# Vision tower on one Trainium2 core: the last two attention batches in pairs of tiles, and layer 1 of the FFN further ahead

## What is computed

```python
h = concatenate([cls_tok, tokens(x) @ W.T])                  # (8, 1025, 64)
e = layernorm(h)
S = (e @ WQ.T) @ (e @ WK.T).T / 8
P = exp(S - max(S)) * where(S == 0, 0, tril)                 # the max runs over the whole row
h = h + (P / (sum(P) + 1e-9)) @ (e @ WV.T)
x2 = layernorm(h)
w = softmax(mean(x2, axis=0) @ Wr + br)                      # one gate per token place, over all 8 batches
t = relu(bn2(relu(bn1(x2 @ W1[e])) @ W2[e]))                 # experts e = 0..7
out = h + sum_e w[:, e] * (t @ Wo[e] + bo[e])
```

## Time and profile before

| | |
|---|---|
| runs | 376.05, 377.1, 378.49 us |
| profiled execution | 379.81 us, its span 377.7 us |
| mean granted TensorE clock | 0.977 |
| TensorE busy | 355.9 us (94%) |
| VectorE busy | 269.9 us (71%) |
| ScalarE busy | 207.6 us (55%) |
| GpSimd busy | 131.6 us (35%) |
| chain that ended last | 83% TensorE, 6% ScalarE, 4% VectorE, 2% DMA |

### The profile page before, as it was taken

One profiled execution on the slowest core, in us unless ns is written; L12 is line 12 of the kernel. 1 busy time (PEld: TensorE's weight loads), 2 busy tenths in 40 slices (PEclk: granted clock), 3 DMA queues, 4 the chain that ended last, 5 costly groups with the idle time before them and its releaser, 6 DMA issues.

```text
span 377.7 us, 8008 instructions
## 1 busy us (share of the span) xinstructions
PE 355.9 (94%) x2690; PEld 171.1 (45%) x2690; DVE 269.9 (71%) x576; ACT 207.6 (55%) x435; POOL 131.6 (35%) x202
## 2 busy tenths in 40 slices
PE   4889999999999999999998999989999999999985
PEld 3555344356356356356355445445544333333321
DVE  3223858979989989989999879886425566566673
ACT  1123655568568468468478486576644545664500
POOL 7060302525625625625716626227306500000000
PEclk9999999999999999999999999996859999999999
DMA  6999651904704604600000000000000011110112
GB/s 154 218 220 187 139 100 39 186 0 93 135 0 101 123 0 102 120 0 0 2 2 1 2 2 1 0 2 0 3 0 3 2 30 28 30 29 1 30 30 56
DMA packets 28992, 20.45 MB, mean 54 GB/s; under 512 B 12280, under 2 KB 28832, under 8 KB 28960
## 3 DMA queue, kind: packets, MB, share of 16 engines
q1 hardware_dynamic: 28352, 19.91, 26.3%
q10 hardware_dynamic: 608, 0.12, 0.2%
HBM read 17.93 MB, written 2.10 MB: 53 GB/s over the span
## 4 chain that ended last, share of the span: by engine, by line
PE 83%; ACT 6%; DVE 4%; issue 4%; DMA 2%; ACTq 1%; DVEq 0%
PE Sp L1370 14%; PE Sp L1638 7%; PE MM L1425 7%; PE PTp L1659 6%; PE MM L1681 6%; PE PTp L1382 6%; PE MM L1301 6%; PE MM L1304 5%; PE MM L1433 3%; DMA c0B<-in_cls_tok_dram 2%; PE MM L1278 2%; PE PTp L1393 2%; PE MM L1282 2%; ACT EP L631 2%; PE PTp L1350 1%
## 5 line engine op out<-in xcount | busy, mean ns | idle before, releaser
L1370 PE MATMUL Sp<-eT,G 64*64 64x512 f32 x512 | 69.5, 603 | 1.7 <-ACT E2T L566 1.5
L424 POOL TENSOR_SCALAR_AFFINE_SELECT EP<-EP 128x128 f32<-128x128 f32 x64 | 22.5, 352 | 104.4 <-ACT EP L628 104.4
L566 ACT ACTIVATE PT<-PTp 128x512 f32<-128x512 f32 (+2 forms) x96 | 42.9, 488 | 28.7 <-PE PTp L1382 22.3
L911 DVE TENSOR_SCALAR_CACHE_REDUCE EP<-Sp,sr 128x1024 f32<-128x1024 f32 x32 | 40.4, 1279 | 3.8 <-PE Sp L1370 3.7
L911 DVE TENSOR_SCALAR_CACHE_REDUCE SN<-Sp,sr 128x1024 f32<-128x1024 f32 x32 | 40.2, 1277 | 1.8 <-PE Sp L1370 1.8
L1370 PEld LDWEIGHTS Sp<-eT,G 64*64 64x64 f32 x512 | 18.8, 132 | 31.0 <-issue 30.8
L920 DVE SCALAR_TENSOR_TENSOR SN<-SN,EP 128x384 f32<-128x384 f32 (+3 forms) x32 | 29.4, 919 | 3.0 <-POOL EP L424 1.9
L1425 PE MATMUL MM<-PT,e 128*64 128x512 f32 (+3 forms) x176 | 31.4, 489 | 0.1
L1638 PE MATMUL Sp<-E2T,W1f 64*64 64x512 f32 x232 | 30.5, 631 | 0.3 <-ACT h L789 0.3
L1199 DVE SCALAR_TENSOR_TENSOR PT<-PTp,negc,XW 128x512 f32<-128x512 f32 x28 | 19.7, 745 | 12.1 <-PE PTp L1659 11.5
L920 DVE SCALAR_TENSOR_TENSOR EP<-EP 128x128 f32<-128x128 f32 (+3 forms) x32 | 25.8, 805 | 1.9 <-ACT EP L631 1.9
(11 more groups left out here) (312 smaller groups left out, 701.1 us busy)
## 6 DMA issues: line engine op xcount, KB each, us to landing
XW<-in_x_dram SPq DMA_DIRECT2D x6, 1024.0 KB, 11.2
X<-in_x_dram SPq DMA_DIRECT2D x6, 1024.0 KB, 10.1
out_dram<-xc SPq DMA_DIRECT2D x8, 256.0 KB, 2.7
XW<-in_x_dram SPq DMA_DIRECT2D x2, 576.0 KB, 7.8
X<-in_x_dram SPq DMA_DIRECT2D x2, 576.0 KB, 14.3
XW<-in_x_dram SPq DMA_DIRECT2D x2, 448.0 KB, 11.8
X<-in_x_dram SPq DMA_DIRECT2D x2, 448.0 KB, 14.0
EP<-in_L_tok_W_dram SPq DMA_DIRECT2D x2, 144.0 KB, 2.8
```

Source lines behind the costliest of these rows:

```text
L566: return act.activation(dst, src, ACT.Copy)
L911: dve.tensor_scalar(W4[t % 4], Sp[t % 2][:, :], -SCALE, sr[q][:, place(t), 0:1], ALU.mult, ALU.min, accum_out=negm[q][:, t:t + 1]).then_in ...
L1370: ins = pe.matmul(Sp[t % 2][64 * s:64 * s + 64, CH * c:CH * c + CH], G[q][rows, 128 * t + 64 * s:128 * t + 64 * s + 64], eT[q][rows, :], **ON)
```

## The change

1. Batches 6 and 7 are written by twos as batches 1 to 5 are. Batch 6 is `pairs` without the token projection. Batch 7 is written out in the same pattern, and takes its tiles in falling order: position p holds tile 7 - p (`tile_of`). The four wide tiles come first, into a buffer `PTd` of their own, and their group is finished first. The last tile has 128 columns. A second small buffer `pzl` serves the row sums of tiles 0 to 3.
2. `PTp0` and `PTp1` become the two halves of one two-bank buffer `PTB`. The first five pairs of layer 1 go through it, between two groups of transposes (`layer1(n, free)` waits until the copies of these are done, and the next `p_turn` waits until the ReLU has read it). Pairs 0 and 1 stand in batch 6, pairs 2 to 5 in batch 7; from pair 5 on `Sp0` and `Sp1` are used, as before.
3. One ReLU instruction covers both banks of a pair (`h1_wide`).
4. `h1` has four buffers instead of two (batch number modulo 4): the old ones, the input buffer `XW`, and `PT[1]`. The gates `WB` move from `XW` to `PTd`, the buffers `t2` to `G`, `SN` and `EP`. At the gates pairs 6 to 11 are done, then pair 12, and the loop takes two and one pairs in batches 1 to 4, two and two in batch 5, two and one in batch 6.
5. Both `bias_rows` run together at the end of batch 5, in `M0`.

The core of the difference:

```diff
-        WB = XW[:, 0:4096].rearrange("p (e s) -> p e s", e=NEXP)
+        PTd = sb("PTd", [128, NT, CH])
+        WB = PTd
...
-              for h_ in (sb("h1", [128, 2 * NPAIR * CH])[:, :], X1[:, :])]
-        t2b = sb("t2b", [128, NPAIR, CH])
+              for h_ in (sb("h1", [128, 2 * NPAIR * CH])[:, :], X1[:, :], XW[:, 0:2 * NPAIR * CH],
+                        PT[1][:, :, :].rearrange("p e s -> p (e s)"))]
...
-        PTp = [pb(f"PTp{i}", [128, CH]) for i in range(2)]
+        PTB = pb("PTB", [128, 2 * CH])
+        PTp = [PTB[:, CH * i:CH * i + CH] for i in range(2)]
...
+        L1_AT = {b: (range(10 + 3 * b, 12 + 3 * b), range(12 + 3 * b, 13 + 3 * b)) for b in range(1, 5)}
+        L1_AT.update({5: (range(25, 27), range(27, 29)), 6: (range(29, 31), range(31, 32)), 7: ((), ())})
...
+        def tile_of(p, down):
+            return NT - 1 - p if down else p
...
+        NMID = 5
+
+        def l1_bank(n):
+            return PTB if n < NMID else Sp[n % 2]
...
-            def h1_first(p, c):
-                act.wait_ge(l1_ready, 2 * p + c + 1)
-                act.activation(h1[0][:, c, p, :], M0, ACT.Relu, bias=c1[:, p:p + 1], scale=s1[:, p:p + 1]).then_inc(h1_done, 1)
+            def h1_wide(n):
+                b, p = n // NPAIR, n % NPAIR
+                act.wait_ge(l1_ready, 2 * n + 2)
+                if b > 3:
+                    act.wait_ge(l2_ready, 8 * (b - 4) + 2 * p + 2)
+                act.activation(h1[b % 4][:, :, p, :], l1_bank(n)[:, :].rearrange("p (c s) -> p c s", c=2), ACT.Relu,
+                               bias=c1[:, p:p + 1], scale=s1[:, p:p + 1]).then_inc(h1_done, 2)
...
-            body(NB - 2, 0, y_next=False, after_pairs=True)
-            body(NB - 1, 1, last=True, y_next=False)
+            pairs(NB - 2, 0, y_next=False, y_more=False)
             b = NB - 1
...
+            def layer1(n, free=None):
+                b, p = n // NPAIR, n % NPAIR
+                pe.wait_ge(e2t_done, b + 1)
+                if n < NMID:
+                    pe.wait_ge(pt_done, free)
                 else:
-                    pe.wait_ge(h1_done, 2 * p + c)
+                    pe.wait_ge(h1_done, 2 * n - 2)
...
+            u_group(b - 1, 0, 1, paired=True)
+            layer1(2, NCH * b + 4)
+
+            score(b, 1, 4, True)
+            score(b, 1, 5, True)
+            pe.wait_ge(h1_done, 6)
+            p_turn(b, 2, paired=True, down=True)
+            p_turn(b, 3, paired=True, down=True)
...
-                layer1_pairs(6 + 4 * b, 2)
+                for n in L1_AT[b][0]:
+                    layer1(n)
                 layer2(b, 2)
                 turn_out(b - 1)
-                layer1_pairs(8 + 4 * b, 2)
+                for n in L1_AT[b][1]:
+                    layer1(n)
```

More of the change, by code:

```diff
@@ L786, in h1_half @@
[L786 to L796 removed]
+                        pt_copy(0, t - 1)
@@ new lines, in _ @@
+            mask(b, 1, 2, True)
+            p0_rest(b - 1, 0, 1)
+            mask(b, 1, 3, True)
+            smax(b, 1, 4, True)
+            smax(b, 1, 5, True)
+            o_norm(b - 1, 1)
+            class_arg(b, 1, 1, 0)
+            mask(b, 1, 4, True)
+            ln2_centre(b - 1)
+            mask(b, 1, 5, True)
+            class_max()
+            smax(b, 1, 6, True)
+            p0_rest(b, 1, 1, 0)
+            smax(b, 1, 7, True)
+            class_arg(b, 1, 0, 1, pzl)
+            ln2_ss(b - 1)
@@ new lines, in _ @@
+            mask(b, 1, 6, True)
+            class_weight()
+            mask(b, 1, 7, True)
+            p0_rest(b, 1, 0, 1, pzl)
+            class_centre()
+            dve.wait_ge(pvs_done, 2 * b + 1)
+            dve.wait_ge(o_ready, 2 * b + 1)
+            for t in range(QG, NT):
+                last_add(t, pz, M1[:, D * (t - QG):D * (t - QG) + D])
+            dve.wait_ge(dve_steps, nth("t_hA", QG))
+            last_centre("A", A)
+            ln2_e(b - 1)
+            dve.wait_ge(pvs_done, 2 * b + 2)
@@ L1515, in body @@
-            def body(b, q, first=False, last=False, y_next=True):
-                late, end = 1 if first else 0, 1 if last else 0
+                pe.wait_ge(h_done, NB)
+                for c in range(2):
+                    for e in range(NEXP):
+                        k = 24 * e + 8 - 8 * c
+                        ins = pe.matmul(M0[0:2 * NEXP, D * c:D * c + D], c2sel[:, k:k + 16], Wof[0:64, e, :],
+                                        start=(e == 0), stop=(e == NEXP - 1))
+                ins.then_inc(pe_steps, 1)
@@ new lines, in _ @@
+            o_group(b - 1, 1)
+            layer1(3, NCH * b + 8)
+            score(b, 1, 6, True)
+            score(b, 1, 7, True)
+            pe.wait_ge(ot_done, 2 * b)
+            for k in range(NT):
+                q0 = 128 * max(0, k - QG)
+                top = D if k % 4 in (1, 2) else 0
+                ins = pe.matmul(M1[top:top + D, q0:CH], e32[1][:, place(k), :], PTd[:, k, q0:CH],
+                                start=(k < 2), stop=(k >= NT - 2), skip_group_check=True)
+            ins.then_inc(u_ready, 1)
```

739 lines of the change are left out of this document (354 added, 385 removed).

## The result

The changed kernel is no faster: 382.36 us in the median of 13 runs, against 376.32 us for the kernel before on the same chip, a ratio of 1.0112 (95% interval 1.0061 to 1.0163). The forecast was 368.7 us, in a range of 363 to 375. The profiled execution took 382.6 us, with a span of 380.9 and a mean granted clock of 0.963 (before 377.7 and 0.977). No run of the changed kernel had a clock above 0.985, and the one that had it was the fastest, 376.38 us.

A forecast was written before the change was run, and what follows sets the result against it. TensorE was taken to bound batches 1 to 5 and the loop, VectorE batches 6 and 7. 379.8 - 9.0 - 1.8 - 0.9 - 2.6 + 0.4 - 0.5 = 365.4, plus 3.3 for low clock: 368.7 us, range 363 to 375.

The forecast's parts named there:

- I take one stretch of 6.82 us as left: 3.3 us.: At the gates: one stretch at 1.2 GHz remains, adding 3.3 us to 365.4; this case had chance 0.40.
- the first fall: First drop to 1.2 GHz before the change, 6.82 us long, behind 2.16 us of TensorE work in 3.59; expected to go.
- the clock stays low as long as now: Rival: small products at batch 7's new end bring the fall; 373.8 to 375.4 us, chance 0.19.
- The price of one low microsecond: Whole kernel: each us at 1.2 GHz with TensorE busy was taken to cost 0.49 us, 8.4 us in all.
- I take the middle of the last two, 256.2: Batches 6 and 7: last mask ends between 254.7 and 257.8, so at 256.2, 3.0 us earlier.
- The slower rival: ReLU of the first five pairs holds up transposes, slack 0.3 to 1.1 us at each place; 381.3 us, chance 0.07.
- This is 9.2 us; with 0.8 us for copies that nothing hides, 10.0.: Last mask to router product: TensorE's work at full clock plus copies, 10.0 us; router product 9.0 us earlier.
- The chain through VectorE, ScalarE and GpSimd is about as long and runs beside it: Last mask to router product: centre, square, sum, power, scale run beside TensorE's work, with no time added.
- VectorE's floor and its waits: Batches 6 and 7: 42.4 us of VectorE work, plus 3.4 us of steady waits or today's 6.5 us.
- the loop is shorter by 2.8 us (forecast 2.7): FFN loop: 19 instead of 22 layer 1 pairs -2.6 us, waits +0.4, a filled wait in batch 6 -0.5.
- bias products and start: End of batch 5: both bias products together put 0.7 us before batch 6 and take 2.1 us out of the batches.
- The rule on idle gaps: Trainium skill: idle gaps throttle the clock; by it alone nothing stays low, 365.4 us, a rival with chance 0.27.

The follow-up runs named there:

- e9: Changed kernel in its own order, products nobody reads put in its large waits (those of e4 and e5 together): 372.96 us, ratio 0.994.
- e3: Changed kernel with both reorderings: `class_exp` moved behind the copies, and pair 4 of layer 1 in a score bank: 375.05 us, ratio 0.987.
- e5: e3 plus four products nobody reads in TensorE's waits behind batch 7: 369.09 us, ratio 0.9809.
- e6: e3 with the wide ReLU of a pair split into two one-bank instructions again: 377.27 us, ratio 1.0032.
- e4: Changed kernel, order left, products nobody reads in its two waits (before position 1's transposes in batch 7, behind pair 4): 378.28 us, ratio 1.01.
- e8: Kernel before, with 1.3 us of products nobody reads meant for its wait at 252.9 us: 381.08 us.
- e1: Changed kernel with `class_exp` moved behind the copies in the list: 378.38 us.
- e7: e3 with two more layer 1 pairs moved from the loop (19 to 17) into TensorE's waits behind batch 7: 372.2 us, ratio 0.9798 from three runs.
- e10: e3 with two 512-column products nobody reads among the narrow products only, the waits at 258 to 264 us left open: 374.38 us, ratio 0.9972.
- e12: Kernel before, with three 512-column products nobody reads between the small products of its gates: 378.58 us, ratio 1.0103.
- e11: e7 with products nobody reads in its two largest waits at the end of batch 7: 368.55 us, ratio 0.9843.

## Why the prediction was wrong

The miss against the profiled run is 382.6 - 368.7 = 13.9 us. It has three main parts, each with a run that shows it.

1. **"I take one stretch of 6.82 us as left: 3.3 us."** This is the step that failed most. The low clock lasted 27.3 us and cost 9.9 us (e9): 6.6 us of the miss. The argument was that the gap ahead of the first fall goes, "since four wide tiles no longer come last". It went, and two others came, of 2.65 and 1.37 us, at places that no row of before shows. I looked only for falls that existed. The rival "the clock stays low as long as now" came nearest: it expected a fall from the new end of batch 7, but from its small products, and with too short a stretch. A longer low clock than today's was in no case. The price of one low microsecond was off the other way: 0.49 in the sum, 0.36 measured (9.9 by 27.3), since slower work fills waits; at the gates 2.3 us of waits in e3 are 0.5 us in the changed kernel.
2. **The waits of batch 7**, 3.2 us (e9 against e5). The step "I take the middle of the last two, 256.2" priced VectorE's waits by the steady batches, and the steady batches go in rising order. That the wide tiles need four chunks in two halves of a buffer, and that an exponential for the class token stands ahead of their copies, could be read in the lists: position by position, what must have left the buffer before the next transposes may start. The slower rival was near it. It took the transposes to be held up by the ReLU, with "a slack of 0.3 to 1.1 us" at five places. One of the five places had this wait (1.37 us); at the other four TensorE did not wait for the ReLU. With both waits taken out and full clock, the masks took 48.05 us against 47.55: VectorE's floor and its waits were sized well.
3. **"This is 9.2 us; with 0.8 us for copies that nothing hides, 10.0."** At full clock the stretch is 14.17 us in e5: 4.2 us more. TensorE works 14.10 - 2.3 = 11.8 us of its own in it, not 9.2. The sum left out the `u_last` of the other three tiles (1.2 us) and what is left of pair 5 (0.6), which in the list stand before the last transposes but in time behind the last mask. It also priced four pairs at 0.88 us each, the time of a pair that another follows, where a pair alone takes 1.02 (0.5 in all). Without the cover it would wait 2.3 us, not 0.8: 0.51, 0.47, 0.42 and 0.92 in e3. "The chain through VectorE, ScalarE and GpSimd is about as long and runs beside it" hid them; but TensorE's list waits for this chain in four places. Nothing there runs simply beside it.

6.6 + 3.2 + 4.2 is 14.0. To this come 0.5 us in the masks, 0.2 at the start and, with the other sign, 0.4 between router product and spreading product (5.52 against 5.9 at full clock) and 0.4 outside the span (1.7 us, before 2.1): 13.9.

**Right, by the marks:** the loop is shorter by 2.8 us (forecast 2.7), with periods of 10.35 us (forecast 10.2); one pair less before it gave 0.86 (0.9); bias products and start 0.9 later (0.7), which may be luck: between profiled runs with the same list up to there, the first scores come at 207.3 to 209.5. The wide ReLU was no cost (e6).

**The rule on idle gaps.** The falls of the changed kernel follow stretches with waits [its windows above]. Covering waits alone removed the first fall in e4, both in e9's profiled run, and e3's in e5. The Trainium skill, "TensorE: Matmul & The Clock Gate", section "HAM oscillation — how this bites in real kernels", holds that idle gaps between bursts throttle the clock and that closing them keeps it up: here these runs agree, by 9.9 us in one kernel, though the waits in the Trainium skill's own case are longer than any here (at most 2.65 us). I had weighed the rule and drawn from it that the falls would become fewer; what it asks is where the *new* order waits. One row speaks against a simple form of it: in e8 a longer wait brought no fall at its place.

**Does the change pay then?** In the kernel as written, no. Without low clock it is 372 us, and the kernel before takes 373.1 to 375.3 us in its runs at a clock of 0.995. With one instruction moved, one pair in another bank, and four products nobody reads, it is 369.1 us, 1.9% under the kernel before (1.55 to 2.27). A part of that is the clock: against the runs of the kernel before at 0.995 in the same set (374.5 to 375.3 us) it is 5.4 to 6.2 us.

**Still open:** why e1 and e3 fall in most and e7 in half of their runs and not in the others; what decides for how long the clock stays low (from 3.4 to 23.9 us) once TensorE is busy again; whether wide products between the narrow ones keep the clock up, which neither e10 nor e12 could show; and whether falling order or twos bring more, which was not tried apart.

## What to carry to other kernels

When an order is changed, walk the new lists position by position and ask of each buffer who must have left it. A wait that was harmless with small tiles first may decide with large ones first. Price the waits twice: once as time, and once as the thin load that can halve TensorE's clock for the next 20 us. Where TensorE must wait ahead of a long dense stretch, put work there, real if there is some, useless if not, into a bank that is free without another wait; in a list that is full already (e12) or behind a wait of its own (e8) it costs more than it brings.

## What the runs showed of the hardware

- The low clock outlasts its cause: after a stretch with 3.31 us of work in 5.20, TensorE was at 1.2 GHz for 23.9 us, with 22.09 of 22.59 us busy. In e5, with the two waits out of the list and the others covered, the clock never fell while TensorE had work, in four runs (0.997 to 1.000).
- The same program has the fall in some runs and not in others (e1: 9 of 10 at 0.975 or less; e3: 8 of 10 at 0.980 or less; e7: 3 of 6; e11: 1 of 6; e5: 0 of 4). One look at one profile can therefore mistake a version by 7 us.
- A ReLU over two banks (128x1024) takes 1.20 us, two over one bank each 2 x 0.775: 0.35 us less ScalarE time per pair.
- VectorE's operation on 128x4 (L963) took 1.21 us at 237.07, where the like takes 0.15 at 250.95. It ended at 238.28, as an addition of 128x512 on GpSimd did (236.15 to 238.26); the mask ahead of it took 1.61 us for 896 columns where the one before it, wider, took 1.21. So VectorE waited, inside its instructions, until GpSimd was done. The kernel before has it too: 1.24 us at 234.78, beside the same addition. In the changed kernel it is 1.06 us of the chain that TensorE's first wait of 2.65 us hangs on. No run here varies it. The rows of VectorE (changed kernel, then the kernel before), and of GpSimd in the changed kernel:

```profile
234.13 1.21 DVE L955 SCALAR_TENSOR_TENSOR EP<-EP 128x1024 f32<-128x1024 f32 x1
...
250.95 0.15 DVE L963 SCALAR_TENSOR_TENSOR pz<-sr,negm 128x4 f32<-128x4 f32 x1
```
```profile
234.78 1.24 DVE L927 SCALAR_TENSOR_TENSOR pz<-sr,negm 128x4 f32<-128x4 f32 x1
```
```profile
236.15 2.11 POOL L486 TENSOR_TENSOR facc<-facc,E2T 128x512 f32<-128x512 f32 x1
```

  The Trainium skill, "GPSIMD Engine Reference", section "Specifications", has an explanation: GpSimd shares its way into SBUF with VectorE, with contention where VectorE's instruction has two SBUF inputs. All these have two, and the trace agrees (0.15 against 1.21 us); in the forecast it had no place.
